# A fused attention and feed-forward block on one core: two extra TensorE products behind each row-maximum unit of blocks 0 and 1

## What is computed

```python
def reference(x, gamma, beta, w_qkv, w1_w, w1_s, ...):     # x: (1, 4096, 256), 16 heads of 16
    xn = layernorm(x) * gamma + beta
    q, k, v = split(xn @ w_qkv.T)
    sim = (q * 16 ** -0.5) @ k.T                           # causal, per head
    x = layernorm(x + softmax(sim) @ v)
    h = silu((x @ w1.T) * w1_s) * ((x @ w2.T) * w2_s)      # 256 -> 1024
    h = gelu((h @ h1.T) * h1_s)
    h = gelu((h @ h2.T) * h2_s)                            # 1024 -> 1024
    return layernorm(x + (h @ w3.T) * w3_s)                # 1024 -> 256
```

## Time and profile before

| what | value |
|---|---|
| median of 3 runs | 2284.06 us (2283.5 to 2284.6) |
| the profiled execution's own time | 2284.38 us |
| its span, first to last instruction | 2282.8 us |
| TensorE busy, share of the span | 99% (2253.1 us, 15594 products) |
| VectorE, ScalarE, GpSimd busy | 76%, 71%, 9% |
| mean granted TensorE clock | 0.997 |

### The profile page before, as it was taken

The page is one execution under the profiler, slowest core; times in us unless marked ns, Lnnn a source line. Parts: engine busy times, 40 slices in busy tenths (PEclk is TensorE's granted clock), DMA queues, the critical chain, the costliest instruction groups (busy, mean ns, idle before and its releaser), DMA issues. The chain is left out here.

```text
span 2282.8 us, 40909 instructions
## 1 busy us (share of the span) xinstructions
PE 2253.1 (99%) x15594; PEld 1394.5 (61%) x15594; DVE 1738.5 (76%) x3748; ACT 1621.0 (71%) x3131; POOL 201.5 (9%) x237
## 2 busy tenths in 40 slices
PE   8999999999999999999999999999999999999998
PEld 5555555555555556555555555554588888888887
DVE  8899998888889897888989898996435445544543
ACT  4677888889999888889989899999723333432332
POOL 3211100011000102000010201001100000000000
PEclk9999999999999999999999999999999999999999
DMA  3110001100000200000020000205410000000000
GB/s 102 31 27 16 5 20 40 38 20 20 20 19 1 59 20 20 20 20 19 1 56 20 20 20 20 77 1 168 151 42 15 5 19 19 10 10 19 15 5 20
DMA packets 72295, 70.22 MB, mean 31 GB/s; under 512 B 41632, under 2 KB 51744, under 8 KB 70688
## 3 DMA queue, kind: packets, MB, share of 16 engines
q1 hardware_dynamic: 67392, 56.03, 9.3%
q0 software_dynamic: 4704, 11.53, 1.7%
HBM read 28.20 MB, written 4.19 MB: 14 GB/s over the span
## 5 line engine op out<-in xcount | busy, mean ns | idle before, releaser
L728 ACT ACTIVATE PR<-bank 128x512 f32<-128x512 f32 (+1 forms) x2176 | 1097.2, 593 | 75.6 <-PE bank L1094 70.6
L822 DVE TENSOR_REDUCE pm<-bank 128x1 f32<-128x512 f32 x1442 | 932.5, 684 | 134.2 <-PE bank L1054 114.9
L1111 PE MATMUL bank<-PR,V 128*17 128x512 f32 (+3 forms) x4608 | 553.2, 562 | 0.3 <-POOL PR L624 0.3
L1089 PE MATMUL bank<-MR,ones 64*128 64x512 f32 (+3 forms) x2304 | 464.7, 383 | 7.1 <-ACT sums L744 4.6
L1499 PE MATMUL bank<-e_hid,e_h_sb 128*128 128x512 f32 x2048 | 466.1, 389 | 0.0
L1499 PEld LDWEIGHTS bank<-e_hid,e_h_sb 128*128 128x128 f32 x2048 | 383.8, 188 | 81.1 <-DVE e_hid L1369 1.5
L1321 ACT ACTIVATE e_tmp<-bank,scales 128x512 f32<-128x512 f32 x128 | 88.3, 690 | 322.8 <-PE bank L1499 322.7
L1089 PEld LDWEIGHTS bank<-MR,ones 64*128 64x128 f32 x2304 | 239.6, 185 | 81.9 <-ACT PR L728 37.1
L825 DVE CUSTOM_DVE_ANT_0 bank<-bank,below 128x256 f32<-128x256 f32 (+3 forms) x512 | 239.9, 514 | 32.0 <-PE bank L1054 30.9
L711 ACT ACTIVATE mx_sb<-bank 128x512 f32<-128x512 f32 x350 | 209.8, 599 | 56.0 <-PE bank L1054 52.1
L1054 PEld LDWEIGHTS bank<-KA,QX 64*128 64x128 f32 x992 | 127.7, 183 | 186.7 <-ACT PR L728 76.9
(11 more groups left out here) (138 smaller groups left out, 1726.3 us busy)
## 6 DMA issues: line engine op xcount, KB each, us to landing
xnT<-in_h_dram SPq DMA_DIRECT2D x8, 1024.0 KB, 4.9
KA<-qk_hi SPq DMA_DIRECT2D x88, 64.0 KB, 2.2
KA<-qk_lo SPq DMA_DIRECT2D x88, 64.0 KB, 2.2
QX<-qk_hi SPq DMA_DIRECT2D x80, 64.0 KB, 2.2
QX<-qk_lo SPq DMA_DIRECT2D x80, 64.0 KB, 2.2
xres<-in_x_dram SPq DMA_DIRECT2D x8, 512.0 KB, 8.1
e_h_sb<-in_h_dram POOLq DMA_DIRECT2D x2, 2048.0 KB, 11.1
e_h_sb<-in_h_dram POOLq DMA_DIRECT2D x1, 4096.0 KB, 23.6
```

Source lines behind the costliest of these rows:

```text
L728: act.activation(PR[:, s % NPB, h, off:QB], ring_bank("score", s, h)[:, off:QB], ACT.Exp).then_inc(exp_done, 1)
L822: dve.reduce_max(pm[:, B % 2, i, a, p, 1 + c:2 + c], bank[:, :], AX.X).then_inc(mx_done, 1)
L1089: pe.matmul(ring_bank("score", s, h)[:, at:at + QB - q], ones[rows(a), p, :], MR[rows(a), B % NM, q:QB], start=True, stop=False)
L1111: last = pe.matmul(ACC[32 * h:32 * h + VW, q:QB], V[:, v_tile(B, tile), GH * (B // NJ % 2) + h, :], PR[:, s % NPB, h, at:at + QB - q], sta ...
```

## The change

Behind each unit of block 0 and block 1 stands a new op `("fill", 2)`: two products of 64 rows, 128 columns of weights and 512 streamed columns, from the Q and K slots of block 0 (both on `rows(0)`), into bank 7. They wait for nothing of their own, signal nothing, and nobody reads what they write, since `av` starts bank 7 anew. There are 24 units, so 48 products and 48 weight loads. The plan of times for the banks counts each product at 213 ns.

```diff
@@ Schedule.__init__, per step
                 units.append(("unit",) + item)
+                if item[0] == 1:
+                    units.append(("fill", 2))
@@ take_banks
+            if op[0] == "fill":
+                now += 213 * op[1]
@@ intro
-        first = [("unit", 0, n) for n in range(len(maxima_of(0)))]
-        second = [("unit", 1, n) for n in range(INTRO_UNITS)]
+        first, second = [], []
+        for n in range(len(maxima_of(0))):
+            first += [("unit", 0, n), ("fill", 2)]
+        for n in range(INTRO_UNITS):
+            second += [("unit", 1, n), ("fill", 2)]
@@ on TensorE
+            def fill(n):
+                for _ in range(n):
+                    pe.matmul(ACC[:, :], q_slot(0)[rows(0), 0, 0:P], k_slot(0)[rows(0), 0, :], start=True, stop=True)
...
+                if op[0] == "fill":
+                    fill(op[1])
```

## The result

| | before | changed |
|---|---|---|
| median of 21 runs | 2284.2 us (2283.5 to 2285.88) | 2287.7 us (2286.64 to 2289.67) |
| ratio of the times | | 1.0016 (95%: 1.001 to 1.0022) |
| the profiled execution's own time | 2284.38 us | 2288.05 us |
| its span | 2282.8 us | 2286.3 us |
| mean granted TensorE clock | 0.997 | 0.997 |

The change costs 3.5 us, 0.15%. It is within the 0.2% that I had called no change, but outside my range (2282.6 to 2287.4) and 3.7 us above the 2284.0 that I forecast. The prediction of the time was wrong.

The account below looks back on a forecast made before the run. TensorE, busy 99% of the span, was taken as the bound, with one half-clock dip in block 1. Block 0's +1.34 us and `v` 1's -1.38 summed to -0.04, giving 2284.0 us, no change; range 2282.6 to 2287.4.

Parts of the forecast that it names:

- The price of a fill: On TensorE, two fills cost 0.43 us, 0.48 at most, at full clock (0.217 each), and 0.86 at half clock.
- Block 0, +1.34: Fills lengthen block 0's two halves by 0.86 and 0.48 us, so block 1's first maximum comes 1.34 us later.
- my upper bound of 1.9: Highest delay allowed for block 0's halves, with 0.25 us for each fill: 1.9 us.
- Block 1 hidden behind VectorE: Up to `v` 1, block 1's fills lie behind VectorE, covered by TensorE's 2.4 us lead, and add nothing.
- The clock stays at 1.00: Fills keep TensorE busy enough in block 1 that the half-clock dip from 40.0 to about 50.2 us disappears.
- my first rival: Clock still falls in block 1 and `v` 1 stays slow: +2.2 us, 2286.2 us; chance 0.18.
- `v` 1 gives back 1.38: At full clock, `v` 1 saves 1.58 and unit 1,11 0.23, less 0.43 for fills: 1.38 us earlier.
- A shift at 60 us stays until the end: After block 1, a shift of the whole list persists unchanged to the end; nothing there waits on its own date.
- Rival 2: Clock falls at 40.0 us and stays low through block 1's fills: +5.1 us, 2289.1 us; chance 0.08.
- rival 4: Block 0's fills hide too and the clock holds: -1.4 us, 2282.7 us; chance 0.05.

Follow-up runs that it names:

- e2: The changed kernel run once more, unaltered, against the kernel before: 2287.49 us, ratio 1.0014.
- e4: The changed kernel with fills behind block 1's units only, against the kernel before: 2283.98 us, ratio 0.9999.
- e9: Block 1's fills only, plus the first 16 product pairs of block 2 issued twice, against the kernel before: 2286.37 us, ratio 1.0009.
- e13: The changed kernel with 160 more TensorE instructions in the warm-up, against the kernel before: 2287.58 us, ratio 1.0014.
- e3: The changed kernel with fills behind block 0's units only, against the kernel before: 2287.27 us, ratio 1.0015.
- e10: The kernel before, no fills, with 96 more TensorE instructions in the warm-up: 2287.06 us, ratio 1.0014 against the kernel before.
- e6: The kernel before with nine warming products instead of five, no fills: 2287.82 us, ratio 1.0016 against the kernel before.
- e12: One fill instead of two behind each unit of block 0, none in block 1, against the kernel before: 2284.57 us, ratio 1.0003.
- e5: Block 1's fills only, on all 128 rows of the array instead of 64, against the kernel before: 2286.37 us, ratio 1.0009.

## Why the prediction was wrong

By its own steps:

- **The price of a fill**: right. 0.23 us between starts, within my 0.217 to 0.24, and no load in the open.
- **Block 0, +1.34**: this term was mis-sized; it measured +2.07, the same in e2 (24.22 - 21.53 = 2.69 and 28.83 - 26.13 = 2.70). I worked the new length out from products alone, 2.32 us, and subtracted an old length read between two loads, with the idle time of the hand-over to the projection in it (the earlier trace rows show 0.26 and 0.24 us there). The new length has one too, 0.36 us. That is 2 x 0.36 = 0.72 of the 0.73 that I missed, and my upper bound of 1.9 didn't hold it either.
- **Block 1 hidden behind VectorE**: right. e4, with only these fills, is not slower, and TensorE still waits for VectorE at the turn of block 1 (1.10 us ahead of 60.12).
- **The clock stays at 1.00**: this step failed as a statement on every execution. It held from 40 to 46 us in every trace with two fills per unit of block 1, but on `v` 1 only in some: in e2, e4, e9 and e13 it held, in the profiled execution of the changed kernel it fell. And in that execution, in e3, e4 and e10 it was low for some time between 59 and 67 us, a place that I had not thought of. My forecast and my first rival are two executions of one kernel. Against the trace of before, the clock with its start is worth +0.84 us in the one (-0.56 at the start, +0.58 on `v` 1, which is 2.25 - 1.67, and +0.8 for the fall at 63) and -0.53 in the other (+0.41, -1.01, and +0.1 in small terms). Neither comes near the -1.38 that I had set against block 0. Nor is this the step that makes the miss: the seven executions at 0.999 have a median of 2287.1 us, 3.1 above the forecast.
- **`v` 1 gives back 1.38**: mis-sized; where the clock held, 1.01 (1.67 to 0.66, e2 and e4). My 1.88 us for `v` 0 runs from its second load on (the earlier trace rows has 15 loads there); `v` 1 with all 16 takes 51.58 - 49.59 = 1.99 us in e2, 0.11 more. The 0.23 us of unit 1,11 did not come at all: from unit 1,0's first load to `v` 1's are 10.28 us before and in e2, and the hand-over ahead of `v` 1 has grown from 0.37 to 0.48. Behind `v` 1 the fills cost 0.46, not 0.43. So 1.58 - 0.11 - 0.46 = 1.01.
- **A shift at 60 us stays until the end**: right for a shift (e6), wrong for the change. It also makes TensorE's program longer, and moves the fetches onto DMAs that ScalarE waits for. That term, +1.1 us, was put at nothing in my sum.

The sum as measured, for the profiled execution at the last block: block 0 +2.07, clock and start +0.84, 383 us +0.53, 766 us +0.57, and -0.08 in drifts between, 3.93 in all. For e2: +2.07, -0.53, +0.48, +0.59, -0.03, 2.58. The median of +3.5 lies between these two.

Rival 2 (the clock low all through block 1) and rival 4 (block 0's fills hide) did not come up in any trace; rival 4 is half right for a single fill, as e12 shows. In rival 2 I counted the fills behind `v` 1 at 0.43 us where at the half clock my own price is 0.86, so its time is 0.4 us too low.

What stays open: which condition decides in an execution whether and when the clock falls. Shown is that one program does either, and that fills behind block 1's units put the fall off or avoid it. That e3 reaches +3.0 us without late steps I put down to the clock, which its trace shows low at 42.6, 49.5 and 63.1 us: seven of its ten executions have a mean of 0.996, where 26 of the kernel before's 31 beside it have 0.997. No run separates this. And how a fetch slows the DMA issues beside it (a shared engine, the queue, or memory) was not tried.

## What to carry to other kernels

Read both lengths with the same ends: if the old one comes from load to load and holds a hand-over, the new one, worked out from products, must hold it too. Extra products are free only as far as they fill a wait that is already there (one per unit in block 0, two per unit where VectorE sets the pace), and a gain in clock counts only when it is there in several executions of the same program. When steps show up far behind an edit, look for a change in the engines' instruction counts: an experiment that pads the count without the edit tells the edit from its length.

## What the runs showed of the hardware

- An instruction fetch of 16 KB (256 instructions of TensorE) coincides with SyncE's DMA issues taking 1.7 to 2.3 us a pair instead of 1.23 at the places shown, and with a transfer under way beside it landing after 3.1 us instead of 2.2. A fetch falls every 2286.3 / 124 = 18 us. Between 80 and 1640 us 12 to 16 of 450 issues take 1.0 to 1.9 us instead of 0.6 in the traces of before and of the changed kernel, all of them beside a fetch, and most cost nothing. Where ScalarE waited for the transfer, the step was 0.3 to 1.2 us.
- Products on one half of the array that reload this same half start 0.23 us apart, their loads of 0.18 us hidden.
- Going over from 64-row to 128-row products, the weight loads stood 0.24 to 0.48 us for issue, and back 0.36 in e5, where units of 512 columns then started 1.10 us apart where the half-array fills would make it 0.69.
- The first load at the full clock came at 8.28, 9.25 and 10.11 us, and the clock fell at 40.0, at 46.3, at 49.1 or not at all in executions of the same two programs. Ahead of the falls at 40.0, 46.3 and 49.1, from 36, 42 and 44 us on, no idle time between weight loads was longer than 0.48 us. In e2 an idle time of 1.10 us stands ahead of 59.52, and the clock held.
